# A graph kernel with another beginning: split edge rows, gathers behind the turned sources alone, weight columns copied by ScalarE

## The reference

```
h = (x - mean(x)) * rsqrt(var(x) + eps) * gamma + beta
a_in  = segment_sum((h @ W_in + b_in)[src] * w1, dst)
a_out = segment_sum((h @ W_out + b_out)[dst] * w2, src)
xi, hh = concat(a_in, a_out) @ W_x2i + b_x2i, h @ W_h2h
gate, new = sigmoid(xi_i + hh_i), tanh(xi_n + hh_n)
x1 = layernorm(x + new + gate * (h - new))
f = (x1 - mean(x1)) / (std(x1) + 1e-4)
out = layernorm(x1 + segment_sum(f[src] * w1, dst) @ W1 + b1)
```

## Time and profile before

| | |
|---|---|
| median of 3 runs | 3756.04 us |
| lowest, highest | 3748.25, 3762.41 us |
| the profiled execution, its own time | 3757.66 us |
| its span, first to last instruction | 3755.9 us |
| mean granted clock of TensorE | 0.862 of full speed |
| busy: PE, DVE, ACT, POOL | 2712.1, 2266.8, 1035.8, 2693.4 us |
| moved by DMA | 638.35 MB, mean 170 GB/s |
| the chain that ended last, by engine | POOL 31%, PE 26%, issue 19%, DMA 10%, DVE 9% |

### The profile page before, as it was taken

The page is one execution under the profiler, slowest core; times in us unless marked ns, Lnnn a source line. Parts: engine busy times, 40 slices in busy tenths (PEclk is TensorE's granted clock), DMA queues, the critical chain, the costliest instruction groups (busy, mean ns, idle before and its releaser), DMA issues.

```text
span 3755.9 us, 65229 instructions
## 1 busy us (share of the span) xinstructions
PE 2712.1 (72%) x13420; PEld 2082.4 (55%) x13420; DVE 2266.8 (60%) x5359; ACT 1035.8 (28%) x3125; POOL 2693.4 (72%) x2754
## 2 busy tenths in 40 slices
PE   2666667777777777769999999985666665655556
PEld 2554454454444444458888888433455555555554
DVE  5787885334433334336777776986566566666657
ACT  1344232333333333324555555540000000000003
POOL 3777565777777777767777775876777777777771
PEclk8888788889889898979999999997878778677779
DMA  3544734666666666658998897443333333333332
GB/s 108 146 141 129 220 103 149 209 203 205 202 206 206 201 206 204 206 158 258 296 294 291 292 293 246 137 137 117 105 103 104 105 105 105 103 104 105 105 105 85
DMA packets 317664, 638.35 MB, mean 170 GB/s; under 512 B 57202, under 2 KB 135455, under 8 KB 317532
## 3 DMA queue, kind: packets, MB, share of 16 engines
q0 software_dynamic: 122112, 335.31, 28.0%
q1 hardware_dynamic: 192932, 298.30, 26.8%
q10 hardware_dynamic: 2488, 3.28, 0.3%
HBM read 479.98 MB, written 156.69 MB: 170 GB/s over the span
## 4 chain that ended last, share of the span: by engine, by line
POOL 31%; PE 26%; issue 19%; DMA 10%; DVE 9%; ACT 2%; SPq 2%; DVEq 1%; ACTq 0%; POOLq 0%
POOL columns L545 10%; PE ps L968 10%; POOL work L545 9%; POOL messages L502 8%; PE ps L811 7%; PE ps L922 3%; POOL work L482 3%; DMA messages<-work,stage 3%; PE ps L1033 2%; DMA work<-place_row 2%; DMA work<-in_x,stage 2%; DVE work L1638 1%; DMA work<-x_table,wh 1%; PE ps L930 1%; DVE work L1637 1%
## 5 line engine op out<-in xcount | busy, mean ns | idle before, releaser
L482 POOL DMA_INDIRECT work<-in_x,stage x832 | 852.4, 1024 | 356.2 <-issue 288.7
L502 POOL DMA_INDIRECT messages<-work,stage x832 | 826.5, 993 | 277.0 <-issue 236.5
L811 PE MATMUL ps<-work 128*128 128x128 f32 x3328 | 488.0, 308 | 212.5 <-ACT work L588 145.2
L1784 DVE TENSOR_TENSOR node_a<-node_a,ps 128x256 f32 x880 | 369.7, 420 | 419.7 <-PE ps L1033 219.3
L811 PEld LDWEIGHTS ps<-work 128*128 128x128 f32 x3328 | 463.4, 220 | 283.2 <-ACT work L588 153.8
L922 PE MATMUL ps<-work 128*128 128x256 f32 x1664 | 481.4, 440 | 153.1 <-DVE work L1488 152.4
L545 POOL DMA_INDIRECT columns<-x_table,wh x480 | 460.2, 959 | 146.2 <-issue 140.8
L636 ACT ACTIVATE work<-ps,columns 128x256 f32<-128x256 f32 x832 | 326.5, 475 | 730.5 <-PE ps L922 607.1
L1033 PE MATMUL ps<-work,columns 128*128 128x128 f32 x1920 | 336.9, 347 | 232.9 <-DMA columns<-x_table,wh 232.9
L922 PEld LDWEIGHTS ps<-work 128*128 128x128 f32 x1664 | 349.1, 218 | 259.6 <-issue 149.2
L545 POOL DMA_INDIRECT work<-x_table,wh x400 | 383.5, 959 | 132.4 <-issue 119.7
(11 more groups left out here) (260 smaller groups left out, 3505.9 us busy)
## 6 DMA issues: line engine op xcount, KB each, us to landing
work<-messages SPq DMA_DIRECT2D x232, 520.0 KB, 5.0
work<-place_row SPq DMA_DIRECT2D x208, 256.0 KB, 4.0
work<-in_x SPq DMA_DIRECT2D x256, 128.0 KB, 3.0
gate_rows<-work SPq DMA_DIRECT2D x49, 384.0 KB
columns<-gate_rows SPq DMA_DIRECT2D x49, 384.0 KB, 3.1
work<-in_x,stage POOLq DMA_INDIRECT x832
messages<-work,stage POOLq DMA_INDIRECT x832, 3.0
messages<-zeros SPq DMA_DIRECT2D x50, 260.0 KB
```

What stands on the lines that cost most here:

```text
L482: nc.gpsimd.indirect_dma_start(out=big[:, s, j, 0:D], out_offset=None, in_=table, in_offset=bass.IndirectOffsetOnAxis(ap=stage[:, s, j:j + ...
L502: nc.gpsimd.indirect_dma_start(out=messages, out_offset=bass.IndirectOffsetOnAxis(ap=stage[:, s, j:j + 1], axis=0), in_=big[:, s, j, :], i ...
L811: last = nc.tensor.matmul(ps[4 + h][:, k * P:(k + 1) * P], big[:, s, j, k * P:(k + 1) * P], hot[:, h, j, :], start=j == 0, stop=j == CPG - 1)
L1784: last = V.tensor_tensor(tile_of(node_a, w), tile_of(node_a, w), ps[2 * (g % LAST_SUMS) + k // 2][:, (k % 2) * D:(k % 2 + 1) * D], ALU.add)
```

## The change

Four things change. The loads of 79 rows go as 64 rows on SP and 15 rows on ACT's queue, and the four lists count two semaphores instead of one, `ends_loaded` for src and dst and `weight_loaded` for the weights; the last store of 106 rows goes as 96 and 10. The zeroing of `node_a` goes from DVE to POOL, with a wait ahead of the first group on DVE. The raw lists get other places (src as float stays in `work`, dst goes to `half_unit` in `node_c`, the places to `slot_f` in `columns`, the weights behind the gathered rows), so that the gathers overwrite only what the turns of src have read: POOL waits for two turns rather than ten and no longer for the round trip of the lows. And the turns are put in another order: src first, ahead of the lows, then the weights into ps4 and ps5 with ACT copying them out, then the places and dst with DVE as before.

```
-        work = sb("work", [P, max(6 * NC + 4096, RING * CPG * MW + 4 * GE + RING * 4 * MW)])
+        X_AT = RING * CPG * MW + 2 * NC
+        work = sb("work", [P, X_AT + 4160])
...
-        raw_place = area(0, [NC])
-        raw = [area((2 + k) * NC, [NC]) for k in range(4)]
+        raw_place = slot_f
+        raw = [area(2 * NC, [NC]), half_unit, area(X_AT - 2 * NC, [NC]), area(X_AT - NC, [NC])]
...
+        edges = ((src, raw_si, "ends_loaded"), (dst, raw_di, "ends_loaded"),
+                 (edge_weight, raw[2], "weight_loaded"), (edge_weight_n2, raw[3], "weight_loaded"))
...
@@ SP
-            for a, to in ((src, raw_si), (dst, raw_di), (edge_weight, raw[2]), (edge_weight_n2, raw[3])):
+            even = full2 // 16 * 16
+            for a, to, loaded in edges:
                 v = to.rearrange("p (h q) -> p h q", h=2)
-                for s, d in ((a[0:P * GE].rearrange("(g q) -> g q", q=GE), v[:, 0, :]),
-                             (a[P * GE:(P + full2) * GE].rearrange("(g q) -> g q", q=GE), v[0:full2, 1, :])):
-                    sp.dma_start(d, s).then_inc(S["edges_loaded"], 16)
+                rows = a[0:(P + full2) * GE].rearrange("(g q) -> g q", q=GE)
+                sp.dma_start(v[:, 0, :], rows[0:P, :]).then_inc(S[loaded], 16)
+                sp.dma_start(v[0:even, 1, :], rows[P:P + even, :]).then_inc(S[loaded], 16)
...
             sp.wait_ge(S["low_tabs"], 32)
-            sp.sem_inc(S["raw_read"], 1)
...
-                    sp.dma_start(out[FULL * P:N, :], result[0:TAIL, s, :]).then_inc(S[f"result_stored{s}"], 16)
+                    for lo, hi in ((0, TAIL // 16 * 16), (TAIL // 16 * 16, TAIL)):
+                        sp.dma_start(out[FULL * P + lo:FULL * P + hi, :], result[lo:hi, s, :]).then_inc(S[f"result_stored{s}"], 16)
...
@@ POOL
+            nc.gpsimd.memset(node_a[:, :, :], 0.0).then_inc(S["constants"], 1)
...
-            pool.wait_ge(S["raw_read"], 1)
-            pool.wait_ge(S["columns_turned"], 10)
+            pool.wait_ge(S["columns_turned"], 2)
             pool.sem_inc(S["may"], 1)
             gather(x, "in", 0, FIRST)
...
@@ ACT
+                act.dma_start(v[even:full2, 1, :],
+                              a[(P + even) * GE:(P + full2) * GE].rearrange("(g q) -> g q", q=GE)).then_inc(S[loaded], 16)
...
-            act.wait_ge(S["edges_loaded"], 16 * 12)
+            act.wait_ge(S["weight_loaded"], 16 * 8)
...
-            act.wait_ge(S["columns_copied"], 10)
+            for n in range(4):
+                act.wait_ge(S["weights_turned"], n + 1)
+                act.sem_inc(S["may"], 1)
+                to = carried[:, n % 2 * NC // 2:(n % 2 + 1) * NC // 2, 1 - n // 2]
+                nc.scalar.activation(to.rearrange("p (g j) -> p g j", j=CPG), ps[4 + n % 2][:, :].rearrange("p (j g) -> p g j", j=CPG),
+                                     ACT.Copy).then_inc(S["weights_copied"], 1)
+            act.wait_ge(S["weights_copied"], 4)
...
@@ PE
+            pe.wait_ge(S["weight_loaded"], 16 * 8)
...
-            pe.wait_ge(S["places"], 1)
-            for n in range(10):
-                v = (raw[0], raw[2], raw[3], raw_place, raw[1])[n // 2]
-                if n >= 2:
-                    pe.wait_ge(S["columns_copied"], n - 1)
+            pe.wait_ge(S["edges_final"], 1)
+
+            def turn(to, v, half, turned):
                 for j in range(CPG):
-                    last = nc.tensor.transpose(ps[6 + n % 2][:, j * P:(j + 1) * P], by_chunk(v)[:, n % 2, j, :], ident[:, :])
-                last.then_inc(S["columns_turned"], 1)
+                    last = nc.tensor.transpose(to[:, j * P:(j + 1) * P], by_chunk(v)[:, half, j, :], ident[:, :])
+                last.then_inc(turned, 1)
+            for n in range(2):
+                turn(ps[6 + n], raw[0], n, S["columns_turned"])
+            for n in range(4):
+                need(pe, S["weights_copied"], n - 1)
+                turn(ps[4 + n % 2], raw[2 + n // 2], n % 2, S["weights_turned"])
+            pe.wait_ge(S["lows"], 1)
+            for n in range(2, 6):
+                pe.wait_ge(S["columns_copied"], n - 1)
+                turn(ps[6 + n % 2], (raw_place, raw[1])[n // 2 - 1], n % 2, S["columns_turned"])
...
@@ DVE
-            V.memset(node_a[:, :, :], 0.0)
-
-            dve.wait_ge(S["edges_loaded"], 16 * 12)
+
+            dve.wait_ge(S["ends_loaded"], 16 * 8)
...
+            dve.sem_inc(S["edges_final"], 1)
+
+            def copy_columns(n, to):
+                hh = n % 2
+                dve.wait_ge(S["columns_turned"], n + 1)
+                V.tensor_copy(to[:, hh * NC // 2:(hh + 1) * NC // 2].rearrange("p (g j) -> p g j", j=CPG),
+                              ps[6 + hh][:, :].rearrange("p (j g) -> p g j", j=CPG)).then_inc(S["columns_copied"], 1)
+            for n in range(2):
+                copy_columns(n, win_b)
+            dve.wait_ge(S["columns_copied"], 2)
+            link(V.tensor_scalar(src_id, win_b, float(N - 1), None, ALU.min))
+            for s in range(RING):
+                stage_in(s, s)
+
             low_high()
...
             dve.sem_inc(S["lows"], 1)
-            dve.sem_inc(S["places"], 1)
-            for n in range(10):
...
-            dve.wait_ge(S["columns_copied"], 10)
+            for n in range(2, 6):
+                copy_columns(n, (place, carried[:, :, 3])[n // 2 - 1])
+            dve.wait_ge(S["columns_copied"], 6)
...
+            dve.wait_ge(S["constants"], 6)
             in_turn(0, first=True)
...
+            dve.wait_ge(S["weights_copied"], 4)
             turn_slots(0, RING * CPG)
```

More of the change, by code:

```diff
@@ L123, in part_c @@
             return flat_c[:, k * NC:(k + n) * NC]
-        raw_si, raw_di = area(0, [NC], I32), area(NC, [NC], I32)
-        raw_place = area(0, [NC])
-        raw = [area((2 + k) * NC, [NC]) for k in range(4)]
         win, mask, scan, rank, half_win, half_unit, upper_half, win_b = (part_c(k) for k in range(8))
@@ L139, in gnn_program @@
         slot, src_id = slot_f.bitcast(I32), src_f.bitcast(I32)
+        raw_si, raw_di = area(0, [NC], I32), area(NC, [NC], I32)
+        raw_place = slot_f
+        raw = [area(2 * NC, [NC]), half_unit, area(X_AT - 2 * NC, [NC]), area(X_AT - NC, [NC])]
         carried = columns[:, 4 * D + 3 * NC:4 * D + 7 * NC].rearrange("p (c k) -> p c k", k=RW)
@@ L214, in gnn_program @@
             for k in range(LAST_ROWS - RING - 1)]
-        xs, xt = area(6 * NC, [RING, 2 * D]), area(6 * NC + 3904, [D])
-        shift_t, bio_t, w_t = area(6 * NC + 2048, [2, P]), area(6 * NC + 2304, [4, P]), area(6 * NC + 2880, [8, P])
+        xs, xt = area(X_AT, [RING, 2 * D]), area(X_AT + 3904, [D])
+        shift_t, bio_t, w_t = area(X_AT + 2048, [2, P]), area(X_AT + 2304, [4, P]), area(X_AT + 2880, [8, P])
         const_row = xs[0:1, 2:4, :]
@@ L436, in _ @@
             over_tiles(sp, result_store, turn=4)
-            sp.wait_ge(S["result_stored0"], 16 * (FULL // 4 + 1))
+            sp.wait_ge(S["result_stored0"], 16 * (FULL // 4 + 2))
             for s in range(1, 4):
@@ L555, in _ @@
             act.wait_ge(S["pads_set"], 1)
-            for a, to in ((src, raw_si), (dst, raw_di), (edge_weight, raw[2]), (edge_weight_n2, raw[3])):
+            even = full2 // 16 * 16
+            for a, to, loaded in edges:
                 v = to.rearrange("p (h q) -> p h q", h=2)
+                act.dma_start(v[even:full2, 1, :],
+                              a[(P + even) * GE:(P + full2) * GE].rearrange("(g q) -> g q", q=GE)).then_inc(S[loaded], 16)
                 act.dma_start(v[full2:full2 + 1, 1, 0:rest],
-                              a[(P + full2) * GE:E].rearrange("(g q) -> g q", g=1)).then_inc(S["edges_loaded"], 16)
-            act.wait_ge(S["edges_loaded"], 16 * 12)
+                              a[(P + full2) * GE:E].rearrange("(g q) -> g q", g=1)).then_inc(S[loaded], 16)
+            act.wait_ge(S["weight_loaded"], 16 * 8)
             for d, s in ((wio[:, :, 0:D], w_in.rearrange("(k p) n -> p k n", p=P)),
```

## The result

The changed kernel took 3714.23 us, the median of four runs (3710.91 to 3726.62), against 3757.38 for the kernel before in the same comparison: 43 us between the medians; the ratio is 0.9896, with a 95% interval of 0.9873 to 0.992, or 30 to 48 us. The forecast was 3726 in a range of 3714 to 3742, from 30.7 us of gain: the median lies at the very edge of the range, 0.23 us inside it. The profiled execution took 3726.62 us with a span of 3724.9: 31.0 us less than the profiled one of before.

The account below looks back on a forecast made before the run. A chain of waits held the beginning and POOL bounded the gather stage. 29.0 us at the 17th gather plus 1.7 at the last store, 30.7 off 3756.04, gave 3725.3, stated as 3726, range 3714 to 3742.

Parts of the forecast that it names:

- Edge loads: At the beginning, src and dst split into 64 and 15 rows land by 7.6 us, at 249 GB/s from 4.2.
- The memset: Node_a's zeroing on POOL runs 3.4 to 14.2 us; DVE's list casts wait for its end, so they start at 14.2.
- The rival without blocking: At the list casts, POOL's memset holds nothing up: casts at 7.6, 37.4 us gained in all, 3719; chance 0.22.
- From T on: After DVE's list casts start (T, 14.2): first gather at T + 11.6, first one-hot T + 27.9, first sum 46.9.
- the full ring: At POOL's 17th gather: POOL is ready at 46.1 but gathers at 47.7, losing 1.6 us.
- The rival in which DVE becomes the bound: In the gather stage, only DVE's 22.2 us count, 24 in all: 3732; chance 0.24 together with a slower memset.
- Cover that was thinner than said: Before the first one-hot (42.1): the lows' DRAM round trip takes at most 9.02 plus 1.45 us, landing at 39.4.
- The other cover: At the turns: ScalarE copies four weight columns at no cost; without cover, at worst four one-microsecond copies before the first scaled group.
- The row split: List loads spread over engines at about 250 GB/s instead of 25; rival without spreading gives 3732, chance 0.04.
- The store: At the kernel's end, the last store as 96 and 10 rows lands at 3753.6 against about 3755.3: 1.7 us.
- The clock of the packed stage: TensorE's clock stays 1.00; slower rival: each 0.01 costs 6.2 us, at 0.93 the kernel takes 3769; chance 0.03.
- absorbed further on: Rival after the gather stage: part of the gain is lost, under 18.8 us left, around 3745; chance 0.08.

Follow-up runs that it names:

- second profile: The changed kernel run again unaltered, its profile at 3.7 ms: 3714.27 us against 3750.64 for the kernel before, ratio 0.9915, span 3711.6.
- weight columns by DVE: Changed kernel with the four weight columns copied by DVE again instead of ScalarE, behind the lows: 3720.09 us in one run.
- gathers late: Changed kernel with POOL again waiting for all six DVE column turns and the returned lows before its first gather: 3728.35 us, ratio 0.9945 to the kernel before.
- zeroing shared: Changed kernel with POOL clearing one half of node_a and ScalarE the other: 3712.91 us against 3750.64 for the kernel before, ratio 0.9906.
- and lows once: Shared-zeroing kernel with the second pair of dst reductions moved into the general case: 3713.73 us against 3752.04 for the kernel before, ratio 0.99.
- the kernel with the rows whole: Changed kernel with the lists loaded as 128 and 79 rows again, all else as changed: 4621.54 us, one run at 4.6 ms.
- rows split only: Kernel before with only lists split into 128, 64, 15 rows and last store into 96, 10: 4606.45 us against 4627.32, ratio 0.9948.

## Why the prediction was right, point by point

**Edge loads.** Expected 7.6 for src and dst, measured 9.07. The rate was as expected (243 GB/s from 4.20 to 9.07), but the sum had src and dst alone in the engines. From 3.20 to 9.07 the transfers moved 1.19 MB (202 GB/s), and the two lists are 0.85 MB: a good 0.3 MB of the weight lists, issued from 4.8 on, went beside them, 1.4 us at that rate. Each SP issue also took up to 0.6 us instead of 0.4. It cost nothing, since the memset was the later one.

**The memset.** The step that I weighed between no wait and a full wait came out as the full wait: the memset ended at 14.05 for 14.2, and the first cast half a microsecond behind it. Doubled, it blocks twice; ended early, not at all. The rows that the step was weighed with (0.4 us of excess beside instructions of 0.7) did not show so long a wait; from the rows alone it was a guess between two bounds that came true. The Trainium skill (SBUF — State Buffer, Who interferes with whom) has it, for a VectorE operation in a two-port mode, as an exclusive lock held for the whole instruction; here that is 5.53 us for a cast of 0.69 and 11.33 for the other one. The rival without blocking (3719) is ruled out in its mechanism, though the measured median (3714.23) lies nearer to its number than to 3726.

**From T on.** First gather at 25.35 for 25.8, one-hot 41.86 for 42.1, first sum 46.70 for 46.9. I had miscounted here: the gather at 76.74 in the earlier trace rows is the 16th. The 17th is this one:

```profile
77.99 0.94 POOL L482 DMA_INDIRECT work<-in_x,stage  x1 [0.30 <-issue]
```

Its shift is 77.99 - 48.03 = 30.0 us instead of 29.0; counted right, the working would have given 30.3, and 32.0 in all. I had POOL lose 1.6 us to the full ring; it lost nothing in the first profile and 1.2 us in the second. But it took 22.7 us from its first gather to the 17th, where it had taken 21.5 before.

**POOL sets the stage.** Four further kernels at 3.7 ms bear it out. The table has the 17th gather, the fixed block of DVE and the distance between them.

| | 17th gather | fixed block | between |
|---|---|---|---|
| before | 77.99 | 362.87 | 284.9 |
| changed, first and second profile | 48.03, 49.37 | 332.97, 332.63 | 284.9, 283.3 |
| weight columns by DVE | 51.01 | 337.21 | 286.2 |
| gathers late | 61.91 | 344.84 | 282.9 |
| zeroing shared | 42.49 | 329.65 | 287.2 |
| and lows once | 43.28 | 327.02 | 283.7 |

Wherever the 17th gather starts between 42 and 78, the block follows 283 to 287 us later. The rival in which DVE becomes the bound would have it follow DVE's one-hot, which is at 41.2 in the kernel with late gathers and 41.9 in the changed one: from there it is 304 us to the block in the one and 291 in the other. That kernel decides, since in the others the one-hot moves together with the gather. The 4 us between the rows of the table are scatter or something not found: the second profile of the change has its 17th gather 1.3 us later than the first and its fixed block 0.3 us earlier.

**Cover that was thinner than said.** I let the lows land at 39.4, 2.7 us before the one-hot. In the first profile they are packed at 41.23, just in time; in the second DVE waits for them (1.57 us) and they hold the one-hot, as the chain of waits shows:

```profile
28.44 11.14 DMA group_row<-dlowi
...
39.60 3.04 DMA low_tab<-group_row
...
42.66 0.23 DVE low_two L1392
...
43.22 0.70 DVE work L1308
```

I took the 9.02 and 1.45 us of the earlier trace rows as the most that they would take; here they are 11.14 and 3.04. That term was mis-sized. It costs 1.4 us at the one-hot of this profile, of which nothing is left at the fixed block, and it is why the lows taken once gave hardly anything at the first sum.

The other cover, ScalarE's for the weight columns, holds in the change: it copies them from 24.98, while DVE is at the lows and places, and TensorE's last turns wait for DVE, not for it. The kernel with the rows whole shows its price once the weight lists are late, some 4.5 us at the one-hot.

**The rest.** The row split works (rivals out by 234 GB/s and by the two kernels with and without it). The store gave 1.7. The clock of the packed stage stayed at 1.00. In the first profile nothing was absorbed further on: the marks stay 27.6 to 30.4 us earlier. The sum, 30.7 us, is 31.0 in that profile, but 44.3 in the second (3755.9 - 3711.6), and the two comparisons have ratios worth 39 and 32 us and medians 43 and 36 us apart; it lies inside both ratios' intervals (30 to 48 and 26 to 38). So the path and its marks were forecast rightly, while at 3.7 ms the medians lie farther apart than the sum, by 6 and 12 us, and what of this is more than scatter the runs don't show. That the first median still fell into the range, by 0.23 us, is luck.

## What to carry to other kernels

Look for stretches at 25 GB/s in the transfer rates, and at the row counts of the loads there: 79 rows went at 25 GB/s, the same rows as 64 and 15, beside loads of 128, at 234. A long memset on GpSimd is not free filler: here it held VectorE's casts inside SBUF until it ended (5.53 and 11.33 us for 0.69), so let it end before the data lands, or give part of it to ScalarE, beside whose write the casts took 0.69. Other VectorE work was not tried beside it; the padding's memsets took 0.48 us each whether a short GpSimd memset ran beside them or not. And where a ring of slots feeds a stage that one engine bounds, measure a change to the beginning at the first instruction after the ring is full, not at the first of each engine; in this kernel that tells what comes later to some 4 us.

## What the runs showed of the hardware that was not expected

A tiny round trip through DRAM is long, and its length varies. From the issue of the write of the lows (1 KB, as 256 values of four bytes) to the issue that waits for it took 9.0, 10.4 and 10.4 us where no gather ran beside it (the kernel before, rows split only, gathers late), and 8.1 to 11.5 where gathers did, so the gathers are not what makes the write long. Reading it back took 1.5 to 2.1 us without gathers and 1.9 to 4.3 with them. In the kernel with the rows whole, where other transfers moved 288 GB/s beside the first half of the write, it took 13.4 us; that these were the reason wasn't tested.

Chips differ much more than the change: the same kernel took 3.75 ms on some and 4.62 ms on others (the kernel before: medians 3750.64 and 4627.32; mean granted clocks of TensorE 0.86 and 0.80). The profiles there have waits that end with no event they know, marked `remote`, of which the 3.7 ms profiles have none, and their waits for known events are longer too. These two are of the changed kernel at 4.6 ms, over the whole span; in its first profile at 3.7 ms the second one is 75.1 us in all:

```profile
DVE node_c L1506 <- remote: 534.4, 75, 15.2
...
POOL work L488 <- DVE stage L1212: 357.1, 98, 23.3
```

(The columns are us in total, times, longest.) The first gather comes at the same time there (25.36), while the gather stage is longer: 323 us from the 17th gather to the fixed block instead of 284. What holds the engines in those gaps wasn't found out.
